# Transformer block on one core: index copies taken out of the expert gathers, recurrence inputs in column groups, another order on the sync engine

## The reference, cut to what matters

```python
# layer 1: attention, softmax over 1024 keys, 16 heads of 16
attn = softmax((q1 @ k_eff1.T + q2 @ k_eff2.T) * scale);  x = x + (attn @ v) @ Wo
# layer 3: recurrence for each channel d, state h of 16
h = einsum('dnm,bdm->bdn', A, h) + Bm[None] * x_t[..., None]
y_t = einsum('dn,bdn->bd', Cm, h) + Dm * x_t
x = x + gelu(layernorm(y)) @ W_out.T + b_out
# layer 4: experts, top 2 of 16
h = relu(einsum('sbd,edh->esbh', x, W1) + b1);  y = einsum('esbh,ehd->esbd', h, W2) + b2
out = einsum('esbd,sbe->sbd', y, cw)      # cw: weights of the two chosen experts, 0 elsewhere
```

## Time and profile before

| what | us |
|---|---|
| median of 3 runs | 1789.2 (1785.7 to 1794.1) |
| the profiled execution | 1793.0 |
| its span, first to last instruction | 1791.3 |

### The profile page before, as it was taken

The page is one execution under the profiler, slowest core; times in us unless marked ns, Lnnn a source line. Parts: engine busy times, 40 slices in busy tenths (PEclk is TensorE's granted clock), DMA queues, the critical chain, the costliest instruction groups (busy, mean ns, idle before and its releaser), DMA issues. The chain is left out here.

```text
span 1791.3 us, 40219 instructions
## 1 busy us (share of the span) xinstructions
PE 1547.0 (86%) x13944; PEld 1022.1 (57%) x13946; DVE 1219.9 (68%) x2169; ACT 986.5 (55%) x2037; POOL 431.4 (24%) x570
## 2 busy tenths in 40 slices
PE   5979999999999999998699967888774399999990
PEld 4843333333333333336588856778673399888880
DVE  6668998999999999922588866666567722222225
ACT  2426887888888888880354412343222255555443
POOL 3146000000000000000012137212221555565550
PEclk9967998999999999998799968999886599999995
DMA  5942233343332323000100001333109422221218
GB/s 179 288 150 32 43 51 48 57 66 57 60 57 44 56 44 56 8 20 19 13 1 0 1 14 49 97 97 97 48 25 334 162 72 64 67 64 61 67 62 284
DMA packets 122481, 135.18 MB, mean 75 GB/s; under 512 B 28820, under 2 KB 93352, under 8 KB 122216
## 3 DMA queue, kind: packets, MB, share of 16 engines
q1 hardware_dynamic: 109576, 107.60, 25.4%
q0 software_dynamic: 7584, 20.72, 3.6%
q10 hardware_dynamic: 5184, 4.98, 0.8%
HBM read 92.23 MB, written 36.04 MB: 72 GB/s over the span
## 5 line engine op out<-in xcount | busy, mean ns | idle before, releaser
L1875 DVE TENSOR_REDUCE mx<-ps 128x1 f32<-128x1024 f32 x512 | 611.9, 1219 | 30.0 <-PE ps L2003 25.8
L1918 ACT ACTIVATE PR<-ps 128x512 f32<-128x512 f32 x1024 | 557.2, 599 | 106.8 <-PE ps L2048 56.0
L2003 PE MATMUL ps<-KQ 48*128 48x512 f32 x1024 | 392.9, 467 | 10.7 <-PEq L246 6.0
L2048 PE MATMUL ps<-KQ 50*128 50x512 f32 x1024 | 381.4, 452 | 4.3 <-DMA KQ<-nmT 4.1
L2032 PE MATMUL ps<-PR,VO 128*32 128x256 f32 x4096 | 332.3, 397 | 9.0 <-ACT PR L1918 8.5
L2048 PEld LDWEIGHTS ps<-KQ 50*128 50x128 f32 x1024 | 157.2, 187 | 223.6 <-ACT PR L1918 201.5
L2032 PEld LDWEIGHTS ps<-PR,VO 128*32 128x32 f32 x4096 | 81.0, 108 | 197.0 <-ACT PR L1918 96.0
L2003 PEld LDWEIGHTS ps<-KQ 48*128 48x128 f32 x1024 | 160.6, 194 | 29.6 <-DVE mx L1875 23.5
L1762 PEld LDWEIGHTS ps<-e_xinT,e_w 128*128 128x128 f32 x1264 | 156.4, 195 | 5.8 <-issue 1.7
L1752 PE MATMUL ps<-eW,e_hiddenT 128*128 x632 | 155.9, 390 | 2.5 <-issue 0.8
L1762 PE MATMUL ps<-e_xinT,e_w 128*128 128x128 f32 x1264 | 157.0, 278 | 1.1 <-ACT e_xinT L1694 1.1
(11 more groups left out here) (276 smaller groups left out, 2194.3 us busy)
## 6 DMA issues: line engine op xcount, KB each, us to landing
qk_parts<-parts SPq DMA_DIRECT2D x8, 2048.0 KB
TB<-toeplitz_lines SPq DMA_DIRECT2D x32, 512.0 KB, 5.8
KQ<-qk_parts SPq DMA_DIRECT2D x96, 128.0 KB, 5.8
KQ<-qk_parts SPq DMA_DIRECT2D x192, 64.0 KB, 5.9
eW<-in_L_ffn_W SPq DMA_DIRECT2D x16, 512.0 KB, 6.5
eW<-in_L_ffn_W SPq DMA_DIRECT2D x8, 1024.0 KB, 12.5
e_got<-expert_outputs SPq DMA_DIRECT2D x16, 512.0 KB, 9.6
X<-in_L_attn_x SPq DMA_DIRECT2D x8, 512.0 KB, 4.4
```

The costliest lines, as they stand in the source:

```text
L1875: nc.vector.tensor_reduce(mx[:, u % RING, h * QT + q:h * QT + q + 1], ps[:, b:b + 2].rearrange("p a n -> p (a n)"), AX, ALU.max, negate=Tr ...
L1918: nc.scalar.activation(PR[:, kt % 2, h], ps[:, st_bank(u, s)], ACT.Exp).then_inc(exp_done, 1)
L2003: made = nc.tensor.matmul(ps[:, max_bank(u, t) + k], of_tile(queries(u % RING), h, q), kq[half(h, KROWS), 0, h % HR, k * BANK:(k + 1) * BA ...
L2048: nc.tensor.matmul(ps[:, st_bank(u, s)], kq[half(h, AROWS), 0, h % HR, kt * P:(kt + 1) * P], queries(u % RING)[half(h, AROWS), qc, h % HR] ...
```

## The change

Four things are changed.

1. Experts: GpSimd's program is written out for all 79 tiles, and each indirect DMA takes its indices from a fixed column of `token` or `y_row`. The copies L1665 and L1674, the waits of GpSimd for itself, and the tiles `index` and `y_index` are gone.
2. Recurrence inputs: for each slot, four products of 32 columns of `KM[.., GT_]` with the 64 inputs of just their two channels, on four column groups of the array, in place of one with 256. The result for a pair of slots is 128x128 instead of 128x512, so one multiplication with `mask2` (two channels in four) and a sum over 2 channels follow.
3. Recurrence kernel k: `Cbd` is 32 columns wide for each slot (the upper 24 zero), and the four slots go to four column groups of the array, into one 128x128 block. `zk`, `k0`, `rowBC` and `dcol` now have 32 partitions for each slot and are shorter along the row. The store of `zk` becomes four DMAs. `rowBC` is loaded by 8 DMAs and `dcol` by 4, after GpSimd has zeroed them (`rows_zeroed`); `dcol` no longer comes by a TensorE turn of `rowsD`. The matrix `mask2` is one more step of GpSimd.
4. Attention, SyncE: in unit u the heads of u-1 come first, then 9 of the 18 loads, then `rows(u, 1)`, then the other 9 loads, then `rows(u + 1, 0)`.

```diff
@@ experts
                     def fetch(k, r):
                         pool.wait_ge(xt_done, k + 1)
-                        pool.sem_inc(fetch_turn, 1)
-                        nc.gpsimd.tensor_copy(index[:, r:r + 1], token[:, ds(k, 1)]).then_inc(index_ready, 1)
-                        pool.wait_ge(index_ready, k + 1)
-                        pool.sem_inc(fetch_turn, 1)
-                        nc.gpsimd.indirect_dma_start(xin[:, r], None, xrows, bass.IndirectOffsetOnAxis(ap=index[:, r:r + 1], axis=0)).then_inc(x_loaded[r], 16)
+                        nc.gpsimd.indirect_dma_start(xin[:, r], None, xrows, bass.IndirectOffsetOnAxis(ap=token[:, k:k + 1].bitcast(U32), axis=0)).then_inc(x_loaded[r], 16)
...
+                    for k in range(MT):
+                        fetch(k, k % AHEAD)
+                        if k >= FIRST:
+                            scatter(k - FIRST, (k - FIRST) % 2)
@@ recurrence, TensorE
-                            last = nc.tensor.matmul(in_bank(G_BANK[p], j), KM[:, z, j, GT_], xs[:, z, j].rearrange("p c t -> p (c t)"), start=True, stop=True, skip_group_check=True)
+                            for i in range(P // TILE):
+                                own = slice(TILE * i, TILE * (i + 1))
+                                last = nc.tensor.matmul(ps[own, G_BANK[p], (j % HS) * TC * NT:(j % HS + 1) * TC * NT], KM[:, z, j, GT_, own],
+                                                        xs[:, z, j, TC * i:TC * (i + 1)].rearrange("p c t -> p (c t)"), start=True, stop=True, skip_group_check=True)
...
-                                        last = nc.tensor.matmul(ps[0:GC, SMALL, s * P:(s + 1) * P], Cbd[:, s], W1[:, s, 0:P], start=True, stop=True, skip_group_check=True)
+                                        last = nc.tensor.matmul(ps[TILE * s:TILE * (s + 1), SMALL, 0:P], Cbd[:, s], W1[:, s, 0:P], start=True, stop=True, skip_group_check=True)
@@ recurrence, VectorE
-                            for j in slots(p):
-                                nc.vector.tensor_tensor(gm[:, j % HS], in_bank(G_BANK[p], j).rearrange("p (c t) -> p c t", c=GC),
-                                                        mask[:].unsqueeze(2).broadcast_to([P, GC, NT]), op=ALU.mult).then_inc(g_steps, 1)
+                            nc.vector.tensor_tensor(gm[:], ps[:, G_BANK[p], 0:HS * TC * NT].rearrange("p (s c t) -> p s c t", s=HS, c=TC),
+                                                    mask2[:].unsqueeze(1).unsqueeze(3).broadcast_to([P, HS, TC, NT]), op=ALU.mult).then_inc(g_steps, 1)
...
-                            nc.vector.tensor_copy(zk[:, z, :, 0:P - 1], small[0:GC, :, 1:P]).then_inc(k_kept, 1)
-                            nc.vector.tensor_copy(zk[:, z, :, P - 1:P], k0[:, ds(SLOT * b, SLOT)].unsqueeze(2)).then_inc(k_kept, 1)
+                            nc.vector.tensor_copy(zk[:, z, 0:P - 1], small[:, 0, 1:P]).then_inc(k_kept, 1)
+                            nc.vector.tensor_copy(zk[:, z, P - 1:P], k0[:, ds(b, 1)]).then_inc(k_kept, 1)
@@ recurrence, SyncE
-                    for s, rows in enumerate((bm_in, cm_in)):
-                        sp.dma_start(rowBC[:, s], rows.rearrange("(g c) n -> c g n", c=GC)).then_inc(rows_loaded, 16)
+                    sp.wait_ge(rows_zeroed, 3)
+                    for j in range(SLOT):
+                        own = slice(TILE * j, TILE * j + GC)
+                        for s, rows in enumerate((bm_in, cm_in)):
+                            sp.dma_start(rowBC[own, s], rows.rearrange("(b j c) n -> j c b n", j=SLOT, c=GC)[j]).then_inc(rows_loaded, 16)
+                        sp.dma_start(dcol[own], dm_in.rearrange("(b j c) -> j c b", j=SLOT, c=GC)[j], allow_slow_non_contiguous=True).then_inc(rows_loaded, 16)
@@ attention, SyncE
-                if u + 2 < UNITS:
-                    sp.wait_ge(st_done, BLOCKS * u)
-                    load_qk(sp, u + 2, (u + 2) % RING)
                 if u > 0:
                     heads(u - 1)
-                rows(u, 1)
+                for some in (range(LOADS // 2), range(LOADS // 2, LOADS)):
+                    if u + 2 < UNITS:
+                        sp.wait_ge(st_done, BLOCKS * u)
+                        load_qk(sp, u + 2, (u + 2) % RING, some)
+                    if some.start == 0:
+                        rows(u, 1)
```

82 lines of the change are left out of this document (39 added, 43 removed).

## The result

The changed kernel takes 1780.5 us (median of 15 runs, 1756.2 to 1817.4); the kernel before took 1793.0 in the same sitting (15 runs). Their ratio is 0.9885, with a 95% interval of 0.9855 to 0.9915: about 1.1% faster, where 1758 us, 2.0%, was forecast. (The ratio is formed from undisturbed executions, nine of the fifteen of the changed kernel, and the profiled execution is one of the other six, 3.8 us above the median; the two medians alone give 0.993.) The profiled execution took 1784.3 us with a span of 1782.4, 8.9 less than the span of before.

A forecast was written before the change was run, and what follows sets the result against it. The prediction took TensorE, its own products and its waits, to bound the kernel. Attention 8.4, recurrence 23.3 and experts 3.1 sum to 34.8 us off 1793.0, forecasting 1758 us, range 1749 to 1769.

The forecast's parts named there:

- SyncE's order, the wait at mid-unit: Attention: maxima rows start 1.1 us earlier, shrinking TensorE's five waits for them; 3.5 us saved, bounds 0 and 4.1.
- The clock behind that wait: Attention, unit 3: products at 1.2 GHz after its 1.61 us wait return to full clock; 4.9 us saved, bounds 0 and 4.9.
- The clock falls anyway: Rival, attention: the clock dip stays, so 0 to 3.5 us saved instead of 8.4; 1763 to 1767 us, chance 0.12.
- slower: Rival, attention: maxima rows queue behind nine fresh loads, 6.5 us more per affected unit; 1832 us at ten units, chance 0.03.
- The lock: Recurrence, L1011: VectorE's copy, held by GpSimd's addition, arrives before it; store and TB loads may go 2 us sooner.
- k on column groups: Recurrence, joint turn: four k products on four column groups take 0.27 us instead of 1.04; 0.75 us saved.
- Inputs: Recurrence, joint turn: input products take 1.1 us instead of 1.89; 0.8 us saved, 0.2 charged for tiling changes.
- Mask and sum: Recurrence, joint turn: VectorE's masked pair takes 0.7 us instead of 1.75, twice a turn; TensorE's waits shrink 2.0 us.
- What is late next in a joint turn: Recurrence: TB loads land by 1154.3, TensorE needs them at 1156.4; it holds by 2 us.
- The other turns: Recurrence: first joint turn 2.2 us shorter, last turn 2.0 shorter (0.5 to 3.5), first turn 1.0 longer.
- Experts, the middle: Experts: TensorE is full, busy 311.81 of 332.20 us, so the 77 other gathers gain nothing.
- Start (1.1) and end: Experts: copy and wait gone before first gather, 1.1 us, and before last scatter; 3.1 us together, bounds 2 and 4.

The follow-up runs named there:

- `columns_only`: Kernel before with only the recurrence's column groups changed, SyncE's order and the experts as before: 1779.8 us, ratio 0.9894.
- `old_order`: Changed kernel with SyncE's attention order of before put back, recurrence and experts still changed: 1766.5 us, ratio 0.9818.
- `turn_back`: Changed kernel plus GpSimd's wait for VectorE's turned maxima, with index copies, their waits and four semaphore increments per tile back in the written-out experts: 1776.4 us.
- `unit0_old`: Changed kernel plus GpSimd's wait for VectorE's turned maxima and TB loads in two pairs, with SyncE's old order in unit 0 alone: 1742.4 us.

## Why the prediction was wrong, point by point

- **SyncE's order, the wait at mid-unit** (3.5 us, bounds 0 and 4.1): right as a mechanism; all 4.1 us went.
- **The clock behind that wait** (4.9 us): right in that the dip went with the wait. It counted the five waits alone, though; the order with GpSimd's wait gives 10.4 us over units 1 to 15, because small losses in other units went too. And the 4.9 us were one execution's: with the same order `columns_only` lost 7.8 us in one unit and `old_order` had no dip. The rival "The clock falls anyway" had said why: there was only one dip to learn from.
- **What was left out of that part**: the failed step is the list of who is moved. The prediction followed heads, loads and rows, and held the eighteen loads only against the rows. They also stood right behind the sums load, which landed late because of them. Before, SyncE issued the sums load at 353.26, just ahead of the eighteen at 353.96, and GpSimd could start at 363.96, 10.7 us later; now at 358.37 and 365.05, 6.7 us. That is 4.0 us less, and only 3.6 us lay between two instructions which nothing ordered. "Each queue that it is moved past" has to include who reads what the moved transfers had delayed. The rival "slower" named the rows behind nine loads, a wait that never came.
- **The lock**: the prediction knew it, from L1011, and used it there only. Here the 0.17 us of the cast became 1.9 to 2.4, always ending with GpSimd's 2.38. The Trainium skill (SBUF — State Buffer, section "SBUF: two separate sides") has the one that starts first keep the shared pair for its whole instruction, if VectorE's is in a 2-port mode or has two inputs in SBUF; in which mode this cast runs, no run shows. In the rest these runs agree: L200 began 0.4 us ahead of the cast at 365.05, and where the cast was first (765.90 against 766.01 in `turn_back`) it took 0.17 us and the step behind it 2.32. At L1011's place the time came out as forecast, 0.14 us, but by luck: VectorE does arrive before GpSimd's addition, and in all seven turns behind the first it meets one of GpSimd's copies into `xs` instead, which began 0.1 to 0.4 us earlier, and isn't held by it. That copy is another operation, and L1023 copies 128x1 where L1011 copied 8x4; which of the two frees it, no run tells.
- **k on column groups**: 0.64 us measured for 0.75. **Inputs**: 0.65 us for x32 instead of 1.1. **Mask and sum**: 0.28 + 0.29 us for 0.7 together. The turn without gaps is 20.63 us, as forecast, and 20.0 where no TB loads run.
- **What is late next in a joint turn**: the failed step. "The TB loads" was right, but only their landing was asked for. It held, as said; in the joint turns TensorE hardly waits for TB. What they delay is TensorE's own instructions, and the clock falls behind the gaps. The six turns gave 143.9 - 133.3 = 10.5 us in place of 20.1 here, and 1.6 to 12.5 in the other six profiles of this program. Without TB loads they gave 21.7.
- **The other turns**: first joint turn 3.3 us shorter (2.2 forecast). First turn 0.5 longer (1.0), with VectorE 4.27 us at the wait for `dcol` (the sign named was 5 or more). Last turn 0.9 shorter (2.0): TB waits of 0.67 and 0.52 us and products at 1.2 GHz took the rest, inside its bounds.
- **Experts, the middle**: the failed step is "TensorE is full". 311.8 us of busy time were read as work. The count of records, 210 where 227 fit into 32 us, says otherwise, and so did GpSimd: its "free" 0.9 us for each indirect DMA was its own wait of 0.79 to 0.82 us in a chain. 19 us were there to be gained, and 3.1 were booked. Start (1.1) and end: the last scatter starts 1736.48 - 1734.75 - 0.97 = 0.76 us behind the one before, waiting for VectorE.
- **The range** of 1749 to 1769 would have held 1757.7, the kernel with the one added wait: there the recurrence gave 7.7 us and not 23.3, the experts from first gather to last scatter 19.4 and not 2.0, and the two errors nearly cancel. That would have been luck.

The fastest version here is the changed kernel with GpSimd's wait and the TB loads in two pairs: 1748.1 us, and 1742.4 with the old order in unit 0 besides, a difference that the two intervals (0.9697 to 0.9783 and 0.9660 to 0.9735) don't separate. Nor do they separate the first from GpSimd's wait alone (0.9715 to 0.9791). All three beat the changed kernel and the one before, `unit0_old` by 3.0% (2.7 to 3.4).

## What to carry to other kernels

When an order of transfers changes, list what lands earlier as well as what lands later, and look at which instructions of GpSimd and VectorE then stand side by side without a semaphore between them; one wait can be worth more than the whole reordering. Read the count of instructions in a stretch beside the busy time: an engine that shows 31.8 of 32 us may be paced by another's list, and the engine whose items follow each other without waiting for anybody is the one that sets the pace. A transfer that lands in time can still cost, if it holds up the fetch of an engine's own instructions. And a stage that differs by 12 us between profiles of the same program is not judged by one of them.

## What the runs showed of the hardware

- A VectorE cast of 128x16 next to a GpSimd product of 128x1024 (both operands in SBUF) took 1.9 to 2.4 us instead of 0.17.
- One such delay, seen by TensorE as a wait of 1.35 to 1.87 us, was followed by 1.2 GHz for 3 to 37 us in four cases and by no fall in two: 1.7 to 17.7 us lost in a unit of 40.5.
- In unit 0 the clock came up between 152 and 182 us from one profile to the next, for no reason that these runs show.
- Packets of the instruction queue were 8 to 13 us apart while 2 MB of TB landed, and 3.7 to 7.9 without it; with the faster program TensorE stood still for up to 2.8 us, and went on 2.3 to 2.8 us after the late packet. With loads of an eighth of the size, at 37 to 48 GB/s, two packets were still 12.1 us apart.
- A semaphore increment between a wait and an indirect DMA cost GpSimd 0.52 us.
